# Stacked contraction of the context keys in the weighted sum, and an expert part with its loops written out

## The reference

```
sim = einsum('bhid,bhjd->bhij', q, k); attn = softmax(sim)
out = einsum('bhij,bhjd->bhid', attn, v)      # the weighted sum over 333 keys
```

## Time and profile before

| | us |
|---|---|
| median of three runs | 1092.27 |
| the profiled execution, whole | 1085.1 |
| its span | 1082.9 |

### The profile page before, as it was taken

How to read it: one execution, slowest core, us unless ns; L and a number is a source line. 1 busy time by engine, 2 the same in 40 slices (tenths; PEclk the granted TensorE clock), 3 DMA queues, 4 the chain that set the end, 5 groups by cost and what they waited for, 6 DMA issues and landing times.

```text
span 1082.9 us, 20863 instructions
## 1 busy us (share of the span) xinstructions
PE 1000.7 (92%) x6878; PEld 935.4 (86%) x6878; DVE 804.7 (74%) x2017; ACT 662.5 (61%) x1714; POOL 521.6 (48%) x830
## 2 busy tenths in 40 slices
PE   5799999999999999999999999999999998299970
PEld 4699999999999999999999999999999898289860
DVE  6877777877787878877887878787878765354526
ACT  5576666666666666666766576657675655145625
POOL 5524353645455545554555354535463534325653
PEclk9899999999999999999999999999999999689985
DMA  7381120112111211122111211121103000575448
GB/s 234 128 245 72 34 95 24 57 33 91 34 51 36 85 42 42 37 72 63 43 37 56 79 42 38 40 94 42 38 17 108 23 33 11 190 230 99 68 49 310
DMA packets 60365, 84.46 MB, mean 78 GB/s; under 512 B 13940, under 2 KB 43688, under 8 KB 60264
## 3 DMA queue, kind: packets, MB, share of 16 engines
q1 hardware_dynamic: 52584, 70.46, 19.5%
q0 software_dynamic: 7680, 12.72, 5.7%
HBM read 44.16 MB, written 38.99 MB: 77 GB/s over the span
## 4 chain that ended last, share of the span: by engine, by line
PE 79%; ACT 8%; DVE 7%; issue 3%; DMA 1%; POOL 1%; ACTq 0%; SPq 0%; DVEq 0%; POOLq 0%
PE ps L563 22%; PE ps L565 21%; PE ps L564 21%; PE ps L590 7%; PE ps L657 3%; PE ps L651 3%; ACT prob L1014 1%; DVE nmx L1431 1%; PE ps L695 1%; ACT fx L1086 1%; DVE cv L1152 1%; ACT k_hi L858 1%; DVE gt L1123 1%; PE ps L681 1%; ACT x2T L912 1%
## 5 line engine op out<-in xcount | busy, mean ns | idle before, releaser
L1639 POOL TENSOR_SCALAR prob<-prob,rinv 128x333 f32<-128x333 f32 x256 | 140.7, 561 | 347.4 <-DVE rinv L1440 346.8
L1009 ACT ACTIVATE oT_hi<-ps 128x256 fp32r<-128x256 f32 x128 | 49.2, 384 | 198.7 <-PE ps L565 198.7
L563 PE MATMUL ps<-kv_lo,w_hi 128*128 128x256 f32 (+1 forms) x512 | 159.0, 310 | 2.9 <-ACT x2T L912 1.0
L565 PE MATMUL ps<-kv_hi,w_hi 128*128 128x256 f32 (+1 forms) x512 | 153.4, 300 | 0.0
L564 PE MATMUL ps<-kv_hi,w_lo 128*128 128x256 f32 (+1 forms) x512 | 153.0, 299 | 0.0
L1014 ACT ACTIVATE prob<-ps,nmx 128x333 f32<-128x333 f32 x256 | 134.7, 536 | 10.5 <-DVE nmx L1431 10.4
L1094 DVE TENSOR_TENSOR pT_lo<-ps,pT_hi 128x512 fp32r<-128x512 f32 (+1 forms) x256 | 130.4, 550 | 0.6 <-ACT pT_hi L1026 0.6
L1431 DVE TENSOR_REDUCE nmx<-ps 128x2 f32<-128x666 f32 x128 | 108.5, 848 | 22.3 <-PE ps L565 21.4
L563 PE MATMUL ps<-pT_lo,v_hi 128*128 128x256 f32 (+1 forms) x384 | 108.5, 282 | 0.9 <-DVE pT_lo L1094 0.9
L590 PE MATMUL ps<-ident,prob 128*128 128x128 f32 (+1 forms) x768 | 107.8, 273 | 1.6 <-DVE oT_lo L1094 1.2
L565 PE MATMUL ps<-pT_hi,v_hi 128*128 128x256 f32 (+1 forms) x384 | 108.3, 282 | 0.0
(11 more groups left out here) (230 smaller groups left out, 3005.7 us busy)
## 6 DMA issues: line engine op xcount, KB each, us to landing
wraw<-in_W SPq DMA_DIRECT2D x14, 512.0 KB, 6.8
vcd_hi<-vst_hi SPq DMA_DIRECT2D x10, 512.0 KB, 2.7
vcd_lo<-vst_lo SPq DMA_DIRECT2D x10, 512.0 KB, 3.6
v_hi<-vcd_hi SPq DMA_DIRECT2D x32, 154.0 KB
v_lo<-vcd_lo SPq DMA_DIRECT2D x32, 154.0 KB
slots<-initr SPq DMA_DIRECT2D x8, 520.0 KB, 7.1
xs<-in_x SPq DMA_DIRECT2D x16, 256.0 KB, 3.8
xts<-in_xT SPq DMA_DIRECT2D x15, 256.0 KB, 3.5
```

Source lines behind the costliest of these rows:

```text
L563: pe.matmul(dst, hi1, lo2, start=first, stop=False, skip_group_check=True)
L565: return pe.matmul(dst, hi1, hi2, start=False, stop=last, skip_group_check=True)
L1009: act.activation(oT_hi[:, h % 2, :], ps[:, AVB, 0:S], ACT.Copy).then_inc(oTh_set, 1)
L1639: pool.tensor_scalar(prob[:, h % 2, t, 0:KEYS], prob[:, h % 2, t, 0:KEYS], rinv[:, h % 2, t:t + 1], 1.0, ALU.mult, ALU.mult).then_inc(norm ...
```

## The change

The third block is filled further. REST = 77 - 32 = 45. The block's rows in v_hi become the 77 hi values and, in rows 77 to 121, the lo values of keys 32 to 76. The rows in v_lo become the 77 hi values again and, in rows 96 to 127, the lo values of keys 0 to 31. pT_hi holds against them the hi probabilities and again those of keys 32 to 76; pT_lo holds the lo probabilities and, in rows 96 to 127, the hi probabilities of keys 0 to 31. Rows 77 to 95 of v_lo and pT_lo are zero. Two passes then contain all three products.

For this POOL copies 45 columns of the scaled probabilities behind column 333 (after waiting for its own scaling), the third block's transposes are 122 wide, ScalarE makes one more copy of 32 rows, SyncE issues four transfers per half in place of two, and VectorE clears the padding at startup. At startup the first values are loaded later. The loops of the expert part are written out, and `need_apart`, a wait that also counted a semaphore when its value was a register, becomes `need`. Buffers move: xrow_b shares the place of initr, and four load semaphores are shared with earlier uses.

```diff
-KROWS = [P, P, CTX]
+REST = CTX - 32
+KROWS = [P, P, CTX + REST]
+PCOL = KEYS + REST
...
-        prob = s1("prob", [P, 2, NT, KCOL])
+        prob = s1("prob", [P, 2, NT, PCOL])
...
-                for d, part in zip(vc_rows, (v_hi, v_lo)):
-                    sp.dma_start(ap(part[0:CTX, 2, c]), d[bass.ds(a, 1)].rearrange("o t n -> (o t) n")[:, c]
-                                 ).then_inc(vc_ld[half], 16)
+                hi, lo = [d[bass.ds(a, 1)].rearrange("o t n -> (o t) n") for d in vc_rows]
+                sp.dma_start(ap(v_hi[0:CTX, 2, c]), hi[:, c]).then_inc(vc_ld[half], 16)
+                sp.dma_start(ap(v_hi[CTX:CTX + REST, 2, c]), lo[32:CTX, c]).then_inc(vc_ld[half], 16)
+                sp.dma_start(ap(v_lo[0:CTX, 2, c]), hi[:, c]).then_inc(vc_ld[half], 16)
+                sp.dma_start(ap(v_lo[96:P, 2, c]), lo[0:32, c]).then_inc(vc_ld[half], 16)
...
-                values(0, 0)
                 next_context(2)
                 keep_context(1)
+                sp.wait_ge(pad_set, 2)
+                values(0, 0)
                 keep_values(1)
...
                     if j == 2:
+                        need(pe, twice_set, m + 1)
                         need(pe, pTl_set, 2 * m)
...
-                for j in range(KT):
-                    r, c = KROWS[j], slice(h * DH, (h + 1) * DH)
-                    last = three(ps[:, AVB, 0:S], v_hi[0:r, j, c], v_lo[0:r, j, c], pT_hi[0:r, j, :], pT_lo[0:r, j, :],
-                                 j == 0, j == KT - 1)
-                last.then_inc(av_mm, 1)
+                c = slice(h * DH, (h + 1) * DH)
+                for j in range(NT):
+                    three(ps[:, AVB, 0:S], v_hi[:, j, c], v_lo[:, j, c], pT_hi[:, j, :], pT_lo[:, j, :], j == 0, False)
+                r = KROWS[2]
+                pe.matmul(ps[:, AVB, 0:S], v_hi[0:r, 2, c], pT_hi[0:r, 2, :], start=False, stop=False,
+                          skip_group_check=True)
+                pe.matmul(ps[:, AVB, 0:S], v_lo[:, 2, c], pT_lo[:, 2, :], start=False, stop=True,
+                          skip_group_check=True).then_inc(av_mm, 1)
...
-            with pe.Fori(1, E // 2) as i:
-
-                inner(2 * i - 1, 1)
-                rows(2 * i, 0, 16 * i)
-                outer(2 * i - 1, 1)
-                inner(2 * i, 0)
-                rows(2 * i + 1, 1, 16 * i + 16)
-                outer(2 * i, 0)
+            for e in range(1, E - 1):
+                u = e % 2
+                inner(e, u)
+                rows(e + 1, 1 - u, 16 * ((e + 1) // 2 + (1 - u)))
+                outer(e, u)
...
-                        act.activation(pT_hi[0:CTX, 2, :], ps[0:CTX, T0 + 1, 0:S], ACT.Copy).then_inc(pTh_set, 1)
+                        act.activation(pT_hi[0:CTX + REST, 2, :], ps[0:CTX + REST, T0 + 1, 0:S], ACT.Copy)
+                        act.activation(pT_lo[96:P, 2, :], ps[0:32, T0 + 1, 0:S], ACT.Copy).then_inc(pTh_set, 1)
...
                 dve.memset(oww[:], 0.0).then_inc(owx_set, 1)
+                dve.memset(ap(pT_lo[64:96, 2, :]), 0.0).then_inc(pad_set, 1)
...
                 unit("q", 0, 0, 0, ps[:, 5, :])
+                dve.wait_ge(w_lo_set, 4)
+                dve.memset(ap(v_lo[64:96, 2, :]), 0.0).then_inc(pad_set, 1)
                 for k in range(1, TAPS):
...
                                                rinv[:, h % 2, t:t + 1], 1.0, ALU.mult, ALU.mult).then_inc(norm_set, 1)
+                        need(pool, norm_set, 2 * n + 2)
+                        pool.tensor_copy(prob[:, h % 2, :, KEYS:PCOL], prob[:, h % 2, :, S + 32:KEYS]).then_inc(twice_set, 1)
...
-            with pool.Fori(1, E // 2) as i:
-                add(2 * i - 1, 1)
-                add(2 * i, 0)
-            add(E - 1, 1)
+            for e in range(1, E):
+                add(e, e % 2)
```

More of the change, by code:

```diff
@@ L146, in build @@
         cvec = s1("cvec", [P, D])
-        initr = s1("initr", [P, ST, ROW])
+        clear = ExitStack()
+        initr = sb("initr", [P, ST, ROW], F32, clear)
+        clear.close()
+        lastrow = ExitStack()
+        xrow_b = sb("xrow_b", [P, NT, ROW], F32, lastrow)
+        lastrow.close()
+        xt_hi = s1("xt_hi", [P, KD, S], F32R)
+        xt_lo = s1("xt_lo", [P, KD, S], F32R)
+        s1("after_initr", [P, ST * ROW - 2 * KD * S])
         kv_hi = [s1(f"kv_hi{i}", [P, KD, KCOL], F32R) for i in range(2)]
@@ L315, in build @@
             sem("fnm_set"), sem("fy_set"), sem("out_st"))
-        def need_apart(eng, sem, value):
-            need(eng, sem, value)
-            if not isinstance(value, int):
-                eng.sem_inc(passed, 1)
         def freed(name, idx, b):
@@ L428, in keep_context @@
                 need(sp, cxl_set, c + 1)
-                need_apart(sp, cx_st, 32 * c)
+                need(sp, cx_st, 32 * c)
                 for d, part in zip(cx_tiles, (cx_hi, cx_lo)):
@@ L435, in keep_values @@
                 need(sp, vcl_set, 2 * c + 2)
-                need_apart(sp, vc_st, 32 * c)
+                need(sp, vc_st, 32 * c)
                 for d, part in zip(vc_tiles, (vst_hi, vst_lo)):
@@ L499, in body @@
                 if "att" in have:
-                    need_apart(sp, av_mm, 8 * b)
+                    need(sp, av_mm, 8 * b)
                     values(b, 1)
@@ L513, in body @@
                 if "nxt" in have:
-                    need_apart(sp, vc_st, 32 * tile + 32)
-                    need_apart(sp, av_mm, 8 * b + 4)
+                    need(sp, vc_st, 32 * tile + 32)
+                    need(sp, av_mm, 8 * b + 4)
                     values(a, 0)
@@ L1129, in unit @@
                     need(dve, slot_set, bb)
-                    need_apart(dve, dots_mm, bb + 1)
+                    need(dve, dots_mm, bb + 1)
                     for t in range(NT):
@@ L1588, in normalised @@
                 a = b + 1
-                need_apart(pool, ars_set, a + 1)
+                need(pool, ars_set, a + 1)
                 for t in range(NT):
@@ L1636, in body @@
                     if "att" in have:
-                        need_apart(pool, rinv_set, n + 1)
+                        need(pool, rinv_set, n + 1)
                         for t in range(NT):
@@ L1648, in body @@
                         need(pool, sc_done, 64 * (b - 1))
-                        need_apart(pool, crs_set, b)
+                        need(pool, crs_set, b)
                         for t in range(NT):
```

49 lines of the change are left out of this document (24 added, 25 removed).

## The result

The kernel after takes 1098.01 us (median of 7 runs, 1096.82 to 1099.8) against 1092.27 for the kernel before in the same set of runs: ratio **1.004**, 95% interval 1.0023 to 1.0057. The two medians alone would give 1.0053, which lies inside that interval. It is slower by 0.4%, where 1089.3 was forecast. A second set of runs gave 1089.89 against 1088.12, ratio **1.0017** (1.0008 to 1.0027). The two intervals just touch.

What follows compares the result with a forecast made beforehand. TensorE's sequence and the stalls inside it were taken to bound the attention part; -11.6 + 3.9 + 2.1 + 0.3 + 2.0 + 0.3 = -3.0 us from 1092.27 gave 1089.3 us, range 1081 to 1094.

Steps and rivals of the forecast that it cites:

- The added copy: ScalarE's 32 x 256 copy behind the pT_hi copies: 0.26 us each, costing 3.9, 2.1 and 0.3 us in all.
- the scan's term: VectorE's scan beside POOL's cx_lo in 7 context batches: delayed by POOL's copy, 0.28 us each, 2.0 us in all.
- Passes: TensorE, one of nine passes per head removed at 0.12 us; 31 of 128 lost to stalls, saving 11.6 us.
- The places of ScalarE's copy: On the path in slot 4 of batches 1 to 15 (3.9 us) and slot 3's stall in eight context batches (2.1 us).
- which hides it: Batches without a context unit: q_hi ends 507.37, VectorE comes at 507.90, so ScalarE's copy costs slot 3 nothing.
- POOL's copy: 128 x 90 copy of scaled probabilities: 0.25 us plus 0.10 wait; TensorE's wait for it hidden by over 3 us.
- Startup: VectorE's clear of 32 x 1024 of v_lo ahead of six taps: 0.3 us cost, ends 0 and 1.1.
- SyncE, the loops: Later first values, four transfers per call instead of two, and expert loops written out on TensorE and POOL: all zero.
- The full gain: Rival: stalls of slots 3 and 4 do not grow, every copy hidden; 15.1 us gained, 1077.2; 0.14 together with half-way.
- The slower outcome: Rival: POOL's copy is long, 1.0 us with its wait, delaying the scan; +3.7 us, 1096.0; chance 0.12.
- half-way form: Rival: 31 passes lost but the added copies hidden; 11.3 us gained, 1081.0; chance 0.14 together with the full gain.
- I take the same from it: The forecast's 3.0 us saving, derived from the profiled 1085.1 us, subtracted from the measured median 1092.27, giving 1089.3.

Runs made afterwards that it cites:

- before_loops: The kernel before with the expert part's loops written out on TensorE and POOL, nothing else; ratio 1.0004 to before.
- after_loopback: The kernel after with TensorE's hardware loop of the expert part put back; ratio 1.0008 to before.
- before_eight: The kernel before with one pass of the third block taken out, nothing else; 1076.48 against 1088.12 us, ratio 0.9897.
- after_late: The kernel after with ScalarE's added copy read from pT_hi and moved back in its queue in slots 0, 2 and 4; 1080.34 us, ratio 0.9932 to before.
- before_level: The kernel before plus ScalarE's 32 x 256 copy, written to rows 0 to 31 of a spare place; 1093.0 us, ratio 1.0044.
- before_shifted: The kernel before plus ScalarE's 32 x 256 copy from rows 0 to 31 to rows 96 to 127 of pT_lo; 1100.16 us, ratio 1.0110.
- hold2_noscatter: The kernel before without POOL's scatters of batches 0 to 14 and the waits for them; 1087.72 us, against 1093.01 for its unedited control.

## Why the prediction was wrong

- **Which step failed.** "The 77 x 256 copy starts at 518.83 and its successor at 519.09, so I take 0.26 us; the ends are 0.26 and that copy's shown 0.38." The added copy takes 0.54, above both ends; x2T starts 0.80 behind the pT_hi copy where 0.52 was forecast, and the query unit waits 0.87 where 0.6 was. The nearest row had the same size and source, but not the move between partitions, and that decides. A row with such a move stood in rows 8: the two ys_x copies of 0.40 each, the second from rows 0 to 15 to rows 64 to 79, are shown as 0.84 together, so they don't overlap. The price enters 15 + 8 = 23 times: 23 x 0.28 = 6.4 us. With 0.54 the sum would have been +3.4, or +1.4 with the scan's term gone as it went; the set without the hold gave 0.0017 x 1088 = +1.8.
- **Passes.** 0.12 each, 31 lost, 11.6: measured by itself 11.6 between medians, 11.2 by the ratio. Right.
- **The places of ScalarE's copy.** Slot 4 of every batch, slot 3 of context batches. Right. "which hides it", of slot 3 in the other batches, was right to 0.05: the cover was 507.90 - 507.37 = 0.53, sufficient for 0.26 and just not for 0.54.
- **POOL's copy.** 0.25 forecast, 0.26 measured; TensorE never waits for it. The scan's delay is real, 0.31 to 0.33 for 0.28 forecast, but it was added to a stall ahead of it that takes it away: an error of 2.0 us in the safe direction.
- **Startup.** The clear took 0.91 us at 41.36 and the six taps behind it 5.60, and TensorE restarted at 49.92 in after. The four profiles of the kernel before restart at 49.45 to 50.26, so a difference of 0.3 can't be told.
- **SyncE, the loops.** Zero, as forecast. The page's rule on a taken branch, which the prediction set against its row, gave something to gain; before_loops and after_loopback show no gain beyond 0.1%.
- **The rivals.** The full gain was ruled out by before_eight (11.6, not 15.4), and POOL's copy was short (0.26). The slower outcome came by a way that none of them named. Of the half-way form's gain (passes lost, copies hidden, 11.3 us) after_late gets 0.0068 x 1092 = 7.4.
- **The comparison.** The forecast subtracted from a profile without the hold and set the result on a median that goes with the hold, "I take the same from it". By the slots, the hold takes some 2.5 us more from after than from before; why is not shown. By the ratio after is 0.004 x 1092 = 4.4 us slower, 7.4 from the forecast's -3.0, and the terms give 6.4 - 2.0 + 0.4 (0.05 in slot 3 of the other batches) + 2.5 = 7.3. That the two agree to 0.1 is luck, since the interval of the ratio alone is 1.9 us to either side.

## What to carry to other kernels

Price an operation by a row that moves data the same way, not only by one of the same size: its distance to its neighbours, not its shown duration, is its price, and the two differ by what overlaps. Before adding an instruction to a queue, ask which of its readers is due first and put it behind the work that others wait for; the same copy cost 0.011 x 1087 = 12 us ahead of them in the kernel before, and behind them the change takes only 0.9932 - 0.9916 = 0.16% more than without it. Read a change slot by slot against a run of each half alone, because two delays that meet at the same wait do not add.

## What the hardware did that was not expected

- A ScalarE copy from PSUM whose rows stay in place (before_level) starts 0.26 us behind its predecessor and lets a ready successor start 0.26 behind it. One that writes rows 0 to 31 to rows 96 to 127 (before_shifted) has 0.40 and 0.40, at a shown duration of 0.37 against 0.36. ut and the second ys_x copy of the kernel before, which change rows too, start 0.02 to 0.03 after their predecessor's end.
- A scan of VectorE that meets a POOL subtraction over SBUF ends 0.53 to 0.54 us after it, whether the two met for 0.22 or for 0.57 us. Where they met for 0.06, it took 0.67 as it does alone.
- Beside POOL's indirect scatters instructions of ScalarE that were ready started 0.2 to 1.4 us late in slot 0, in some sets of runs and not in others; in such a set, with the scatters left out, they did not (hold2_noscatter). The kernel before has spans of 1090.8 and 1091.6 us with it, and of 1082.9 and 1086.8 without.
